# Batch 0 of a Mamba and mixture-of-experts layer, dealt anew over its 16 steps

## What is computed

```python
xn = _layernorm(x)
# Mamba, per batch
xz = (xn * rsqrt(mean(xn * xn) + eps) * norm_w) @ in_proj_w.T      # 256 + 256 channels
u = silu(conv4(x_s) + conv_b)
x_dbc = u @ x_proj_w.T                                             # 8 dt, 16 B, 16 C
delta = softplus(dt_raw @ dt_proj_w.T + dt_proj_b)
for t: h = exp(delta_t * A) * h + (delta_t * u_t) * B_t            # 256 channels x 16 states
       y_t = sum(h * C_t)
y = (y + u * D) * silu(z) @ out_proj_w.T + xn
# experts, per token
top_w, sel = top_k(xn @ w_router.T, 2); top_w = softmax(top_w)
out += gates[:, e] * ((silu(xn @ w_gate[e]) * (xn @ w_up[e])) @ w_down[e])
return x + y + out
```

## Time and profile before

| | us |
|---|---|
| median of 3 runs (lowest, highest) | 624.93 (624.63, 625.41) |
| profiled execution | 624.32, its span 622.5 |
| busy in the span: VectorE, TensorE, GpSimd, ScalarE | 591.6, 543.6, 510.4, 455.7 |
| batch 0, first scan to batch 1's first scan | 35.1 to 128.8 |
| mean granted TensorE clock, share of 2.4 GHz | 0.967 |

### The profile page before, as it was taken

The page is one execution under the profiler, slowest core; times in us unless marked ns, Lnnn a source line. Parts: engine busy times, 40 slices in busy tenths (PEclk is TensorE's granted clock), DMA queues, the critical chain, the costliest instruction groups (busy, mean ns, idle before and its releaser), DMA issues.

```text
span 622.5 us, 11479 instructions
## 1 busy us (share of the span) xinstructions
PE 543.6 (87%) x3554; PEld 424.7 (68%) x3554; DVE 591.6 (95%) x852; ACT 455.7 (73%) x916; POOL 510.4 (82%) x481
## 2 busy tenths in 40 slices
PE   5989878898988998989989899899899696869887
PEld 2377766656887777868788677877787464748564
DVE  6989969999999999999999999999999998999997
ACT  1798786139866798578876698767985589969781
POOL 5797159459999999998999989999998978875673
PEclk9979878879999999999999999999999999997999
DMA  7430109724877777978778888588884465322364
GB/s 218 133 109 0 73 2 217 266 76 167 265 263 252 259 281 247 307 241 279 262 244 280 279 306 284 167 301 259 281 274 152 153 217 202 98 93 92 83 131 90
DMA packets 60893, 122.99 MB, mean 198 GB/s; under 512 B 8218, under 2 KB 41378, under 8 KB 53794
## 3 DMA queue, kind: packets, MB, share of 16 engines
q1 hardware_dynamic: 53826, 112.42, 53.9%
q0 software_dynamic: 6288, 9.52, 6.7%
q10 hardware_dynamic: 720, 0.33, 0.3%
HBM read 112.77 MB, written 9.47 MB: 196 GB/s over the span
## 4 chain that ended last, share of the span: by engine, by line
PE 32%; DVE 20%; ACT 15%; issue 14%; POOL 13%; DMA 6%; DVEq 0%; ACTq 0%; POOLq 0%
DVE bank L1134 8%; POOL dbu L921 7%; PE bank L1421 5%; PE bank L1572 5%; DVE h_sb L1151 5%; DMA xs<-xn_rows,src 4%; PE bank L1586 3%; PE bank L1455 3%; PE bank L1580 3%; ACT dbu L531 3%; ACT da L503 3%; POOL xs L908 3%; PE bank L1478 2%; ACT bank L515 2%; PE bank L1384 2%
## 5 line engine op out<-in xcount | busy, mean ns | idle before, releaser
L921 POOL TENSOR_TENSOR dbu<-du,xn_all 128x512 f32<-128x512 f32 x172 | 215.6, 1277 | 21.5 <-DVE bank L1134 20.1
L1134 DVE TENSOR_TENSOR_SCAN bank<-bank,dbu 128x512 f32<-128x512 f32 x170 | 207.5, 1223 | 2.7 <-POOL dbu L921 1.6
L1151 DVE TENSOR_TENSOR h_sb<-bank,xh_all 128x512 f32<-128x512 f32 x240 | 159.6, 679 | 1.2
L515 ACT ACTIVATE bank<-delta,a_sb 128x512 f32<-128x512 f32 x170 | 116.7, 688 | 44.3 <-DVE h_sb L1151 39.6
L1421 PE MATMUL bank<-id_sb,h_sb 128*128 128x128 f32 x992 | 135.7, 282 | 12.4 <-DVE h_sb L1151 9.9
L1421 PEld LDWEIGHTS bank<-id_sb,h_sb 128*128 128x128 f32 x992 | 116.4, 146 | 23.4 <-DVE h_sb L1151 16.5
L1134 DVE TENSOR_TENSOR_SCAN bank<-da,bank 128x512 f32<-128x512 f32 x82 | 96.7, 1215 | 14.8 <-PE bank L1384 10.0
L1572 PEld LDWEIGHTS bank<-wd_sb,hid 117*128 117x128 f32 (+1 forms) x432 | 54.7, 190 | 49.2 <-DVE hid L1185 25.2
L908 POOL DMA_INDIRECT xs<-xn_rows,src x72 | 70.8, 984 | 12.4 <-issue 9.4
L1572 PE MATMUL bank<-wd_sb,hid 117*128 117x128 f32 (+1 forms) x432 | 64.0, 284 | 18.8 <-ACT xT L692 17.3
L531 ACT ACTIVATE dbu<-du_t,bc_sb 128x256 f32<-128x256 f32 x164 | 69.5, 497 | 12.1 <-PE bank L1384 8.0
(11 more groups left out here) (197 smaller groups left out, 894.4 us busy)
## 6 DMA issues: line engine op xcount, KB each, us to landing
xh_all<-b_rows SPq DMA_DIRECT2D x30, 1024.0 KB
xn_all<-b_rows SPq DMA_DIRECT2D x25, 1024.0 KB
wgu_sb<-in_w_gu SPq DMA_DIRECT2D x72, 352.0 KB
wd_sb<-in_w_dn SPq DMA_DIRECT2D x72, 192.0 KB
y_slots<-ys SPq DMA_DIRECT2D x72, 64.0 KB
xn_rows<-xn_all SPq DMA_DIRECT2D x2, 1040.0 KB, 10.2
out<-x_sb SPq DMA_DIRECT2D x7, 256.0 KB
x_sb<-in_x SPq DMA_DIRECT2D x2, 640.0 KB, 5.9
```

Source lines behind the costliest of these rows:

```text
L515: nc.scalar.activation(bank_of(b, m)[:, :], delta[b % 2][:, hf, :], ACT.Exp, scale=a_sb[:, hf, k:k + 1]).then_inc(s["da_rdy"], 1)
L921: nc.gpsimd.tensor_tensor(dbu[k % 2][:, hf, :], du[b % 2][:, hf, :], b_ring[c % 2][:, k % CH, :], ALU.mult).then_inc(s["dbu_p"], 1)
L1134: nc.vector.tensor_tensor_scan(at, da_of(n)[:, hf, :] if n in IN_SBUF else at, inp, 0.0, ALU.mult, ALU.add).then_inc(s["h_rdy"], 1)
L1151: nc.vector.tensor_tensor(h_sb[k % 2][:, hf, :], bank_of(b, 2 * k + hf)[:, :], row, ALU.mult).then_inc(s["p_rdy"], 1)
```

## The change

It deals the side work of batch 0 out over other steps. On TensorE both halves of dbu are turned one step ahead in steps 0 to 2 (before, in step 0 alone), `input_turn(0, 0)` stands ahead of `logits(0)` and `xh_turn(3)`, three `keep` calls go, `rows(1)` moves from step 5 to 7, the step-size matmuls from step 7 to steps 8 and 9, the second part of `skip` from 8 to 12, and the convolutions of batch 2 one step later. On ScalarE the ranks' copy stands first in step 9, the totals' copy behind one `magnitudes`, and the step-size passes are spread over steps 8 to 12. VectorE makes the last four late rows in step 2 and takes `unit(2, hf)` in steps 12 and 15, behind the one-hots. GpSimd does the slot arithmetic ahead of the second `raise_sum`, splits the tile keys, and waits for the one-hots (`hi_rdy`) ahead of `softplus`, `input_scale` and batch 1's first product.

```diff
--- before.py
+++ after.py
@@ -43,7 +43,7 @@
     NXS = 5
     NW = 4
     ND = 3
-    TURNED, SKIPPED0 = 11, (7, 8)
+    TURNED, SKIPPED0 = 11, (7, 12)
     LN_EPS = 1e-5
     RMS_EPS = float(np.finfo(np.float32).eps)
 
@@ -218,12 +218,12 @@
 
         HOT_STEP = {12: (0, 1), 13: (2, 3), 14: (4, 5), 15: (6, 7)}
         MAP_STEP = {13: (0, 1), 14: (2, 3), 15: (4, 5)}
-        LOGITS_AT = {0: (3,), 3: (4,), 4: (5,), 6: (6, 7)}
-        LATE_ROWS = {1: (24, 28), 4: (28, 32)}
+        LOGITS_AT = {0: (2,), 3: (3,), 4: (4,), 5: (5,), 6: (6, 7)}
+        LATE_ROWS = {1: (24, 28), 2: (28, 32)}
 
         def b_turn(k):
 
-            return {0: 4, 1: 5, 3: 6, 5: 7}.get(k)
+            return {0: 4, 3: 5, 4: 6, 5: 7}.get(k)
 
         BY_PE = [k for k in range(1, S)] + [6 * S + k for k in (3, 5, 6, 7, 8, 9, 10, 11, 12, 13, 14, 15)] + [7 * S + k for k in range(2, S)]
         BY_POOL = [n for n in range(S, NB * S) if n not in BY_PE]
@@ -544,6 +544,9 @@
 
             def step0(k):
 
+                if k == 9:
+                    ranks_out()
+                    spread_choices()
                 if k + 2 < S:
                     scaled(k + 2)
                 if k in z_step(0):
@@ -556,21 +559,23 @@
                     half_tanh(1, 1)
                 if b_turn(k) is not None:
                     xh_out(b_turn(k))
-                if k == 6:
+                if k == 7:
                     rows(1)
-                if k in (7, 8):
-                    magnitudes(1, k - 7)
-                    vanishing(1, k - 7)
+                if k in (8, 9):
+                    magnitudes(1, k - 8)
                 if k == 8:
+                    totals_out()
+                if k in (8, 9):
+                    vanishing(1, k - 8)
+                if k == 10:
                     rounded(1)
+                if k == 11:
                     corrected(1)
-                    totals_out()
+                    half_tanh(2, 0)
+                if k == 12:
                     logarithm(1)
-                    ranks_out()
-                if k == 9:
-                    spread_choices()
-                if k in (11, 14):
-                    half_tanh(2, k // 14)
+                if k == 15:
+                    half_tanh(2, 1)
 
             def step(b, k):
 
@@ -866,8 +871,7 @@
             rt(nc.gpsimd.tensor_tensor(kk[:, :], m2[:, :], m1[:, :], ALU.subtract))
             nc.gpsimd.tensor_tensor(kk[:, :], kk[:, :], irms[:, :], ALU.mult).then_inc(s["top_rdy"], 1)
 
-            for hf in range(NH):
-                raise_sum(pool, nc.gpsimd, 1, hf)
+            raise_sum(pool, nc.gpsimd, 1, 0)
             pool.wait_ge(s["rk_out"], 1)
             pool.wait_ge(s["ones"], 6)
             e0, e1 = [v[:, E:] for v in ends]
@@ -891,15 +895,23 @@
             rt(nc.gpsimd.tensor_scalar(lo[:, :], hi[:, :], -float(P), 0.0, ALU.mult, ALU.add))
             nc.gpsimd.tensor_tensor(lo16[:, :], lo[:, :], slotf[:, :], ALU.add).then_inc(s["lohi_rdy"], 1)
             nc.gpsimd.tensor_copy(hi16[:, :], hi[:, :]).then_inc(s["lohi_rdy"], 1)
+            def tile_keys(e0, e1):
+
+                for e in range(e0, e1):
+                    rt(nc.gpsimd.tensor_scalar(tkey[:, :, e], lanes_sb[0:1, 0:NJ], ends[1][0:1, E + e:E + e + 1], 1.0,
+                                               ALU.is_ge, ALU.mult))
+
+            raise_sum(pool, nc.gpsimd, 1, 1)
+            tile_keys(0, E // 2)
             for hf in range(NH):
                 correct(pool, nc.gpsimd, 1, hf)
+            pool.wait_ge(s["hi_rdy"], 2)
             softplus(pool, nc.gpsimd, 1, 1)
-            input_scale(pool, nc.gpsimd, 1, 1)
-            for e in range(E):
-                rt(nc.gpsimd.tensor_scalar(tkey[:, :, e], lanes_sb[0:1, 0:NJ], ends[1][0:1, E + e:E + e + 1], 1.0,
-                                           ALU.is_ge, ALU.mult))
+            tile_keys(E // 2, E)
             tree(tsum[:, :], tkey, tred4, tred2, ALU.add)
             nc.gpsimd.tensor_scalar(texp[:, 0:NJ], tsum[:, :], float(E - 1), None, ALU.min).then_inc(s["texp_rdy"], 1)
+            pool.wait_ge(s["hi_rdy"], 4)
+            input_scale(pool, nc.gpsimd, 1, 1)
 
             def load(j):
 
@@ -984,6 +996,7 @@
                     gathered(b0, c, t)
 
             pool.wait_ge(s["dbu_rdy"], 2 * (S - 2))
+            pool.wait_ge(s["hi_rdy"], 6)
             scaled(S)
 
             def first_loads(k):
@@ -1208,14 +1221,14 @@
                     unit(1, 1)
                 if k == 7:
                     choices()
-                if k in (11, 14):
-                    unit(2, k // 14)
                 if k in z_step(0):
                     z_gate(0, k)
                 if k == 10:
                     weights()
                 for g in HOT_STEP.get(k, ()):
                     one_hots(g)
+                if k in (12, 15):
+                    unit(2, k // 15)
 
             def step(b, k):
                 j = tile(b * S + k)
@@ -1588,38 +1601,35 @@
 
             def step0(k):
 
-                if k > 1:
+                if k > 3:
                     dbu_turn(0, k, (1,))
                 if k > 0:
                     accumulate(k - 1)
                 if k + 1 < S:
-                    dbu_turn(0, k + 1, (0, 1) if k == 0 else (0,))
+                    dbu_turn(0, k + 1, (0, 1) if k < 3 else (0,))
                 for g in MAP_STEP.get(k, ()):
                     inverse(g)
                 if k in (1, 2):
                     conv(1, 1, (2 * k - 2, 2 * k - 1))
-                if k == 5:
+                if k == 7:
                     rows(1)
+                if k in (8, 9):
+                    steps_mm(1, k - 8)
                 if k in SKIPPED0:
                     skip(0, (SKIPPED0.index(k),))
                 if k == 8:
                     totals()
                     ranking()
-                if k in (9, 10):
-                    conv(2, 0, (2 * k - 18, 2 * k - 17))
-                if k in (12, 13):
-                    conv(2, 1, (2 * k - 24, 2 * k - 23))
+                if k in (10, 11):
+                    conv(2, 0, (2 * k - 20, 2 * k - 19))
+                if k in (13, 14):
+                    conv(2, 1, (2 * k - 26, 2 * k - 25))
                 if k + 1 in z_step(0):
                     z_mm(0, k)
                 if b_turn(k) is not None:
                     xh_turn(b_turn(k))
                 for i in LOGITS_AT.get(k, ()):
                     logits(i)
-                if k == 7:
-                    steps_mm(1, 0)
-                    steps_mm(1, 1)
-                if k in (0, 4):
-                    keep(LGB[:, 2 * C - 2 * H + 2 * E:])
                 if k >= 12:
                     keep(MAP[:, 2 * NJ:], k == 12)
                     keep(MAP[:, 2 * NJ:], False)
@@ -1710,12 +1720,10 @@
             conv(1, 0, (0,))
             columns(0)
             conv(1, 0, (1, 2, 3))
+            input_turn(0, 0)
             logits(0)
             xh_turn(3)
-            input_turn(0, 0)
             logits(1)
-            logits(2)
-            keep(LGB[:, 2 * C - 2 * H + 2 * E:])
             for k in range(S):
                 step0(k)
             for b in range(1, NB):
```

## The result

The changed kernel took 626.27 us (median of 20 runs), the kernel before 624.13 beside it (20 runs): a ratio of 1.0038, interval 1.0021 to 1.0054. It is slower by a little, where 7.1 us less were forecast. Its profiled execution took 626.47 us, span 624.7.

What follows compares the result with a forecast made beforehand. VectorE was taken to bound the kernel, full in the later batches. 1.8 + 4.0 + 0.3 + 0.5 - 0.3 + 0.8 = 7.1 us off the profiled 624.32 gave 617.2, as a median 617.8 us, range 615.5 to 620.5 (0.66).

Steps and rivals of the forecast that it cites:

- steps 0 to 3: Batch 0's start: transposes ahead of the convolution and a keep removed shorten VectorE's waits at step 2; gain 1.8 us, bounds -0.3 to 3.0.
- The range: Total time of 614.0 to 622.3 us, taking in the unknown costs; the narrower forecast, 615.5 to 620.5, had chance 0.66.
- Rival (4): Slower: without three keeps TensorE stays at 1.2 GHz through steps 3 to 7, 2.9 us a step; four make 629; chance 0.07.
- The signs: Wrong if: clock 0.50 after 50 us, L669 tanh wait above 1 us, step 15's scan waiting for transposes, batch 1 longer.
- the case of the early clock's fall: Batch 0's start: TensorE's clock falls early, so logits and transposes take about 1.5 us more, partly covered; gain 1.4 us.
- Step 9: Batch 0: an earlier totals' copy cuts VectorE's wait ahead of the second scan from 5.76 to 1.7 us; gain 4.0.
- the bound of 5.3: Upper bound in us of the gain in step 9, if the ranking's matmuls run at 2.4 GHz.
- The z gate's tanh: Step 13, ScalarE: ends at about 102.0 us, VectorE comes for it at 101.8; loss 0.3 us, bounds 0 to 1.5.
- The one-hots: Batch 0: waits on `hi_rdy` push GpSimd's products behind pairs of one-hots, freeing step 14's; gain 0.8 us, bounds -1 to 2.5.
- the later batches as long as before: Sign that the forecast is right: batches behind batch 0 keep their length, so time won in batch 0 reaches the end.
- rival (2): The clock is kind: 3.0 at the start, ranking at 2.4 GHz, one more microsecond of contention gone: 613.3 us; chance 0.08.
- The 620.7 in the sentence on the table load: Time in us if ScalarE's table load costs the skill page's 2.7 us: z gate 2.8 us later, loss 3.

Runs made afterwards that it cites:

- rows in step 4: The changed kernel with the last four late rows of batch 0 back in step 4: 615.8 us beside 621.3, 0.9912 of the kernel before.
- two-input rows: The changed kernel with step 2's four rows made by an instruction taking the scale as a second tensor: 1.0059 of the kernel before.
- pauses: The changed kernel with GpSimd waiting for the end of each residual sum ahead of the next: 0.9956 of the kernel before.
- small sums: The changed kernel with each GpSimd residual sum cut into four of 128 columns, without waits between them: 0.9916 of the kernel before.

## Why the prediction was wrong, point by point

- **The step that failed** is one sentence of the part on steps 0 to 3: "The four late `xh` rows that move from step 4 to step 2 cost VectorE the same there." They cost 7.89 and 7.87 us in two profiles, in place of 1.1, so a term put at nothing was a loss of 6.8 us. The order of time of GpSimd in the kernel before has the row that speaks against it (seven sums in 8.05 us from 48.41 us), and it stands in none of the prediction's rows. The section of the Trainium skill that I named (SBUF — State Buffer, "Who interferes with whom") lists `tensor_scalar`, the form of the rows, among those that can contend with GpSimd. I applied its rule to the edit that spoke of GpSimd and forgot it for a move from one step to another.
- **The range** had 2.5 us for this kind of meeting, as bounds on the one-hots alone, worked out from one meeting of 0.8 us. No term allowed for an instruction that loses again and again: 6.8 us.
- **Rival (4)** named the right sign for another mechanism. TensorE's clock did fall in steps 3 and 4 (granted 0.50 from 57 to 63 us), but behind a hole of 6 us in TensorE's own work that the rows had made, and the time was lost on VectorE. That the sign came out as in this rival is chance.
- **The signs** that the prediction named said wrong in four places: step 2's wait of 1.51 us, a granted clock of 0.50 after 50 us, batch 1's first scan at 128.7 us, and a longer batch 1.
- **Steps 0 to 3**: 1.8 forecast. The waits at step 2 fell from 3.02 to 1.51 or 1.64 us in the profiles of the change. Over all fourteen profiles with the new order there were two cases: in ten the granted clock was 0.50 from 42 to 46 us and 1.5 to 1.6 us of the waits stayed, as in the case of the early clock's fall (1.4 gained); in four (rows in step 4, two-input rows, pauses, small sums) it was 1.00 there and nothing was left (the upper bound, 3.0). Right in size.
- **Step 9**: a wait of 1.7 forecast, 0.98 and 2.21 in the change's two profiles. In the other kernels with this order it was 0.8 to 1.0 us in five profiles, in which the ranking's first two matmuls took 0.70 us together, 2.2 to 2.4 in six, in which they took 1.22, and 1.6 in one. So the size follows TensorE's clock, as the bound of 5.3 had it; undoing this part cost 4.7 us for all it contains, where 5.3 were in the sum. Right. The two matmuls in the change's first profile, then in its second:

```profile
82.86 0.70 PE L1371 MATMUL bank<-sel,before_sb 128*128 128x256 f32 x2 [0.26 <-ACT totc L479]
```

```profile
83.34 1.22 PE L1371 MATMUL bank<-sel,before_sb 128*128 128x256 f32 x2 [0.26 <-ACT totc L479]
```

- **The z gate's tanh** was ready before VectorE asked: no wait, where 0.3 stood in the sum. It came at 108.51 us, behind a table load of 1.28 us, as worked out.
- **The one-hots**: step 14's pair took 2.9 us as said (3.7 before), but in step 12 the `correct` calls made it 4.8 against 4.0. The 0.8 forecast was about zero against the kernel before, though without the waits the new order would lose 1.8 more in batch 0. VectorE's order of time shows the two in step 12 that met GpSimd:

```profile
100.62 1.45 DVE L1106 TENSOR_TENSOR lo_oh<-lanes_sb,lo 128x1024 f16<-128x1024 f16 x1
102.00 1.54 DVE L1107 TENSOR_TENSOR hi_val<-lanes_sb,hi 128x576 f16<-128x576 f16 x1
```

- **The sum** without the collision was 7.1; the kernels without it measure 5.2 to 6.2 us under the kernel before (7 with more keeps). The sign "the later batches as long as before" held for batches 2 to 5: from gate to gate batches 2 to 4 take 72.9 to 73.6 us each, but for one of 74.2 and one of 74.4, and batch 5 69.3 to 70.0, whenever they begin.
- **Slips in the working** that change no term: the parts of rival (2) give 614.3, not 613.3 (3.0 for 1.8, 5.3 for 4.0, 1 more). Rival (4)'s 23.81 us of TensorE work, doubled, exceed the stretch of 24.70 by 22.9 us, not 20. The 620.7 in the sentence on the table load comes out at 620.5 to 620.6.
- **Open**: the changed kernel measured 1.0038 (1.0021 to 1.0054) and 1.0006 (0.9977 to 1.0034), while batch 0's own balance, 6.7 won and 6.6 lost, gives 1.000. The longer batch 1 in some executions is part of it; how often it comes to either kernel was not measured. The end differs too: from the gate behind batch 5 to the last one it took 119.9 to 120.7 us in the four profiles of one chip, on which the kernel before takes 621.3 us, and 121.8 to 125.0 in the others. No run was made to explain that.

The version that beats both is the change with GpSimd's sums held until the rows are made: 0.9907 and 0.9901, or 0.9881 with one more keep in three steps, which can't be told from it.

## What to carry to other kernels

Before an instruction of VectorE moves, look up what GpSimd runs at its new place, not only what its own engine and queue do there; a job of long GpSimd instructions without pauses can hold a short VectorE instruction until the job ends, while scans that read PSUM pass beside it. If such a job has slack, hold it behind the short one by a wait, or cut it into short instructions. And when waits fall and the time doesn't, compare the busy time of the same instructions: the 7.1 us of the held instruction counted as busy, and no list of waits shows them.

## What the runs showed of the hardware that I had not expected

- One VectorE instruction of 128 columns (0.33 us alone) lasted 7.1 us beside GpSimd's sums of 512 columns, and 8.4 us in its two-input form, though there it had begun ahead of the first sum. With short pauses between the sums one got in for each; beside sums or scalings of 128 columns back to back it lost little (groups of 1.61 and 1.25 us). VectorE's scans lost nothing beside the long sums (2.33 to 2.37 us a pair).
- Two profiles of one kernel had TensorE's low clock at different places: batch 1 of 72.8 and 75.3 us for one kernel, 75.2 and 72.8 for the other.
- A `keep`, a matmul that only occupies TensorE, can do harm where the clock has fallen all the same: 2.08 us at 1.2 GHz, ahead of work that others wait for.
